# A two-layer graph network kernel: all first-pass dense chunks moved into stage one, layer 0's second half turned into one transposed pass, half of the dst ids looked up

## The reference

```python
h = jnp.maximum(_layernorm(x, axis=-1), 0.0)
x = x + _L0_gnn_ref(h, edge_index, edge_attr_3, edge_weight, ...)   # x + h + out @ w_out
h = jnp.maximum(_layernorm(x, axis=-1), 0.0)
x = x + _L1_gnn_ref(h, ..., src, dst)                               # three layers over (row, col)
...
proj = jnp.einsum('nf,hfg->nhg', x, w_proj)
delta = proj[sender] - proj[receiver]
radial_logits = jnp.einsum('ehf,hf->eh', delta, radial_score) - radial_distance_scale * edge_len[:, None]
tangential_logits = jnp.einsum('ehf,hf->eh', delta, tangential_score)
alpha = e / s[receiver]
return jax.ops.segment_sum(alpha[:, :, None] * delta, receiver, num_segments=num_nodes)
```

## Time and profile before

| | |
|---|---|
| median of 3 runs | 3198.97 us (3197.86 to 3202.41) |
| span of the profiled execution | 3197.3 us (its own time is not listed apart; the median stands 1.7 us above the span) |
| busy: PE, PE weight load | 1780.0 us (56%), 1443.3 us (45%) |
| busy: DVE, ACT, POOL | 2195.2 us (69%), 1068.3 us (33%), 1913.7 us (60%) |
| chain that ended last | POOL 48%, issue 18%, DVE 13%, PE 12% |
| mean granted PE clock | 0.687 of full speed |

### The profile page before, as it was taken

How to read it: one execution, slowest core, us unless ns; L and a number is a source line. 1 busy time by engine, 2 the same in 40 slices (tenths; PEclk the granted TensorE clock), 3 DMA queues, 4 the chain that set the end, 5 groups by cost and what they waited for, 6 DMA issues and landing times.

```text
span 3197.3 us, 34323 instructions
## 1 busy us (share of the span) xinstructions
PE 1780.0 (56%) x8972; PEld 1443.3 (45%) x8972; DVE 2195.2 (69%) x5951; ACT 1068.3 (33%) x2292; POOL 1913.7 (60%) x1844
## 2 busy tenths in 40 slices
PE   1124444441399986653665654665665656655663
PEld 0023333331299975542454433453444544544442
DVE  6748888887877744434555553897866988766775
ACT  0024444442144420001333323553444644443221
POOL 0057777777888017776777775017773017773776
PEclk9975555565555555556777776897888987787555
DMA  0023332231122212214222211233332333333543
GB/s 7 3 54 82 84 88 82 83 86 41 41 86 86 83 60 69 71 50 96 62 63 61 64 40 34 70 85 96 98 104 64 88 88 94 102 98 84 126 119 85
DMA packets 283933, 238.03 MB, mean 74 GB/s; under 512 B 161125, under 2 KB 207611, under 8 KB 283637
## 3 DMA queue, kind: packets, MB, share of 16 engines
q1 hardware_dynamic: 226933, 196.13, 21.4%
q0 software_dynamic: 56832, 40.05, 5.5%
HBM read 163.62 MB, written 84.20 MB: 78 GB/s over the span
## 4 chain that ended last, share of the span: by engine, by line
POOL 48%; issue 18%; DVE 13%; PE 12%; DVEq 4%; DMA 2%; SPq 1%; ACT 1%; POOLq 0%; ACTq 0%
POOL big L1003 13%; POOL G L994 12%; POOL regs L1845 7%; POOL out L1010 6%; POOL regs L1854 5%; PE bank L923 5%; POOL x_after_layer L647 5%; DVE den L1271 3%; PE bank L916 3%; DVE big L1285 2%; DVE big L1591 2%; PE bank L872 1%; DVEq L1590 1%; PE bank L1451 1%; DVEq L1273 1%
## 5 line engine op out<-in xcount | busy, mean ns | idle before, releaser
L1003 POOL DMA_INDIRECT big<-layer_rows,late x392 | 425.9, 1087 | 305.8 <-SPq L1075 186.9
L1845 POOL DMA_INDIRECT regs<-in_x,G x200 | 213.8, 1069 | 234.8 <-DVEq L1711 174.1
L1451 PE MATMUL bank<-regs,SQ 99*128 99x256 bf16 x1764 | 274.8, 319 | 84.2 <-ACT SQ L1357 77.7
L647 POOL DMA_INDIRECT x_after_layer<-G,idx_s x200 | 197.0, 985 | 198.0 <-DVEq L808 135.9
L1870 POOL DMA_INDIRECT farf<-dst_float,VAL x196 | 252.8, 1290 | 59.7 <-issue 59.7
L1451 PEld LDWEIGHTS bank<-regs,SQ 99*128 99x128 bf16 x1764 | 189.3, 112 | 152.8 <-ACT SQ L1357 102.7
L1010 POOL DMA_INDIRECT out<-G,scat_i x196 | 194.7, 993 | 104.4 <-issue 61.4
L1854 POOL DMA_INDIRECT regs<-in_x,G x200 | 211.2, 1056 | 70.2 <-issue 59.7
L1271 DVE SCALAR_TENSOR_TENSOR den<-steps,late,bank 128x256 f32<-128x256 f32 x588 | 245.2, 472 | 9.6 <-PE bank L1451 9.3
L994 POOL DMA_INDIRECT G<-x_after_layer,own_i x196 | 200.6, 1023 | 69.2 <-issue 61.0
L994 POOL DMA_INDIRECT G<-x_after_layer,far_i x196 | 198.5, 1013 | 66.5 <-issue 66.5
(11 more groups left out here) (416 smaller groups left out, 5745.7 us busy)
## 6 DMA issues: line engine op xcount, KB each, us to landing
regs<-x_after_layer SPq DMA_DIRECT2D x96, 256.0 KB, 3.2
out<-regs SPq DMA_DIRECT2D x96, 256.0 KB, 2.1
XC<-row_of_far_degree SPq DMA_DIRECT2D x147, 128.0 KB, 3.4
den<-in_x SPq DMA_DIRECT2D x50, 256.0 KB, 2.7
x_after_layer<-den SPq DMA_DIRECT2D x50, 256.0 KB, 2.0
regs<-tile_nodes SPq DMA_DIRECT2D x50, 256.0 KB, 3.2
layer_rows<-TS SPq DMA_DIRECT2D x98, 128.0 KB, 2.0
regs<-in_x SPq DMA_DIRECT2D x46, 256.0 KB, 2.8
```

The lines of the kernel that those rows point to most:

```text
L647: g.indirect_dma_start(x1_d, bass.IndirectOffsetOnAxis(ap=idx_s[:, b, k:k + 1], axis=0), G[:, b, k, 0, :], None, bounds_check=top, oob_is_ ...
L1003: ahead(g, l, REVERSED, lambda u, l=l: g.indirect_dma_start(far[:, tile_of(u // C, u % C), :], None, xt_d[l - 1], bass.IndirectOffsetOnAxi ...
L1451: ins = pe.matmul(bank[2 + 2 * b + k // 2][:, (k % 2) * 256:(k % 2) * 256 + 256], OH[b][0:RB1 + 1, k * P:(k + 1) * P], TAB[0:RB1 + 1, part ...
L1845: g.indirect_dma_start(GR[:, c % DEEP, k, 0, :], None, a["x"], bass.IndirectOffsetOnAxis(ap=own0[:, c * C + k:c * C + k + 1], axis=0), bou ...
```

## The change

Line numbers of the changed program are its own. The parts:

1. **Dense chunks.** RUN_W is gone and RUN_A has all 98 chunks. Step c of stage one takes `d0` = chunk 2c - 1 and begins `d1` = chunk 2c, which it finishes in step c + 1. Chunks whose number is a multiple of 4 (24 of them, `by_row`) are handled row by row on ACT: eight Square activations of 64 columns with an accumulated sum, one Sqrt, and eight Relu activations with a scale and a bias of their own. DVE then only sums, makes a small reciprocal and product, and adds.
2. **One turned pass.** The weigh pass and the scatter pass become one of 50 steps. The projection is done with `wm` as the stationary side: two matmuls of 512 moving columns, giving 64 features x 512 edge slots. On that turned layout one `tensor_tensor_scan` with a 0/1 mask, in place in PSUM, forms the running sum of each node with the carry of the chunk before; limiting, the projection with w_out (four small matmuls), and the sum with the own rows follow, and POOL scatters from `big2` with the ids in `scat_i`. Same-node matrix, tile ends, carry step and second turn are gone, and so are their DMAs.
3. **dst ids.** POOL fetches 24 of 49 chunks (96 indirect DMAs). The other 25 are looked up inside the pass: every second step ACT makes four one-hot tiles, PE does 16 matmuls of 98 columns, DVE four picks.

```diff
-RUN_IDS = [[*range(NCH)], [*range(NCH, DCH + 2)], [*range(49)], [*range(49, DCH + 2)]]
+RUN_IDS = [[*range(DCH + 2)], [*range(49)], [*range(49, DCH + 2)]]
+FETCHED = 24
+
+
+def dense_of_step(c):
+
+    return (2 * c - 1 if c else 0, 2 * c if 0 < c < NCH - 1 else None)
...
+        def by_row(tag, c):
+            return tag is RUN_A and c > 0 and c % 4 == 0
...
+        def run_second(v, tag, c):
+            n, (_, _, Q_, st), (name, i) = run_parts(tag, c), run_buf(tag, c), lane(tag, c)
+            v.wait_ge(signal(f"{name}_sq"), i + 1)
+            if by_row(tag, c):
+                v.reciprocal(st[0:n, 2], st[0:n, 2])
+                v.drain()
+                ins = v.scalar_tensor_tensor(st[0:n, 1], st[0:n, 0], -1.0 / F, st[0:n, 2], ALU.mult, ALU.mult)
...
+        def run_square(s_, tag, c):
+            n, (X_, C_, Q_, st), (name, i) = run_parts(tag, c), run_buf(tag, c), lane(tag, c)
+            s_.wait_ge(signal(f"{name}_cen"), i + 1)
+            if by_row(tag, c):
+                for r in range(RW):
+                    s_.activation(Q_[0:n, r], X_[0:n, r], ACT.Square, bias=st[0:n, 0, r:r + 1], scale=-float(F), accum_out=st[0:n, 1, r:r + 1])
+                s_.drain()
+                ins = s_.activation(st[0:n, 2], st[0:n, 1], ACT.Sqrt, bias=eps_c[0:n, :], scale=1.0 / F ** 3)
...
+            if by_row(tag, c):
+                for r in range(RW):
+                    ins = s_.activation(C_[0:n, r], X_[0:n, r], ACT.Relu, bias=st[0:n, 1, r:r + 1], scale=st[0:n, 2, r:r + 1])
...
+                norm_first(v, "g", b, rows.rearrange("p c d f -> p (c d) f"))
+                if before:
+                    run_second(v, RUN_A, before)
+                run_first(v, RUN_A, d0)
+                norm_second(v, "g", c, b)
+                run_second(v, RUN_A, d0)
+                norm_third(v, "g", c, b)
...
+                run_third(v, RUN_A, d0)
                 look_dve(v, c + AHEAD)
-                dense_second(v, RUN_A, c, b, P, run_buf(RUN_A, c))
                 if c:
                     scored(c - 1)
-            dense_third(v, RUN_A, NCH - 1, 1, P, run_buf(RUN_A, NCH - 1))
+                if before:
+                    run_third(v, RUN_A, before)
+                if d1:
+                    run_first(v, RUN_A, d1)
...
+            def scan(c):
+                b = c % 2
+                v.wait_ge(signal(f"n_mask{c % 4}"), 16 * (c // 4 + 1))
+                v.wait_ge(signal("m_mm"), c + 1)
+                v.tensor_tensor_scan(bank[4 + b][0:F, :], MB[c % 4], bank[4 + b][0:F, :], CARRY[1 - b] if c else 0.0, ALU.mult, ALU.add).then_inc(signal("n_scan"), 1)
+                v.drain()
+
+            def guard(c):
+                b = c % 2
+                if c >= 2:
+                    v.wait_ge(signal("n_proj"), c - 1)
+                RS = bank[4 + b][0:F, :]
+                v.tensor_copy(CARRY[b], RS[:, 511:512])
+                v.tensor_scalar(GH[b], RS, 0.0, HUGE, ALU.max, ALU.min)
+                v.drain()
+                v.tensor_scalar(RS, RS, 0.0, -HUGE, ALU.min, ALU.max)
+                v.drain()
+                v.tensor_tensor(GH[b], GH[b], RS, ALU.add).then_inc(signal("n_safe"), 1)
...
+            for i in range(NCH + 4):
+                if i + 1 < NCH:
+                    weigh(i + 1, (i + 1) % 2, (i + 1) // 2)
+                if 0 <= i - 2 < NCH:
+                    scan(i - 2)
+                    guard(i - 2)
+                if 0 <= i - 4 < NCH:
+                    renew(i - 4)
+                if i >= 2 and i % 2 == 0 and i // 2 - 1 < len(LOOKED):
+                    seek_dst_dve(v, i // 2 - 1)
...
+                for q in range(2):
+                    ins = pe.matmul(bank[4 + b][0:F, :], wm[:, q, :], ZTs[b][:, q * 512:(q + 1) * 512], start=(q == 0), stop=(q == 1))
+                ins.then_inc(signal("m_mm"), 1)
...
+            staged(NCH, [(0, turn_weighed), (1, project), (3, out_proj), (0, seek)])
```

More of the change, by code:

```diff
@@ L376, in run_need @@
             k = c % DEPTH
-            before = sum(len(range(k, len(ids), DEPTH)) for ids in RUN_IDS[:RUN_IDS.index(tag[2])])
+            before = sum(len(range(k, len(ids), DEPTH)) for ids in RUN_IDS[:"abc".index(tag[0])])
             return 16 * (before + c // DEPTH + 1)
[L380 to L386, removed]
@@ new lines, in seek_dst_act @@
+        def seek_dst_act(s_, e):
+            b = e % 2
+            s_.wait_ge(signal(f"q_in{b}"), 16 * (NCH // 2 + e // 2 + 1))
+            if e >= 2:
+                s_.wait_ge(signal("dl_mm"), e - 1)
+            for h in range(2):
+                s_.activation(SQD[h], EIDD[b], ACT.Square, bias=hotb[:, h:h + 1])
+            s_.drain()
+            for h in range(2):
+                ins = s_.activation(GED[b][h], SQD[h], ACT.Relu, bias=hotb[:, 2:3], scale=-1.0)
+            ins.then_inc(signal("dl_hot"), 1)
@@ new lines, in seek_dst_pe @@
+        def seek_dst_pe(pe, e):
+            b = e % 2
+            pe.wait_ge(signal("dl_hot"), e + 1)
+            if e:
+                pe.wait_ge(signal("dl_sel"), e)
+            for k in range(C):
+                for h in range(2):
+                    for part in range(2):
+                        ins = pe.matmul(bank[3][:, k * COLS:(k + 1) * COLS], GED[b][h][:, k * P:(k + 1) * P], LTD[:, h, part, :], start=(h + part == 0), stop=(h + part == 2))
+            ins.then_inc(signal("dl_mm"), 1)
@@ L641, in L0_pool, with seek_dst_dve @@
+        def seek_dst_dve(v, e):
+            v.wait_ge(signal("dl_mm"), e + 1)
+            for k in range(C):
+                u = C * LOOKED[e] + k
+                ins = v.scalar_tensor_tensor(PICKD[k], steps[:, 0:COLS], VAL0[:, u:u + 1], bank[3][:, k * COLS:(k + 1) * COLS], ALU.is_equal, ALU.mult, accum_out=farf[:, u:u + 1])
+            ins.then_inc(signal("dl_sel"), 1)
         def L0_pool(g, top):
-            def step(c, b, j):
+            run_stored(g, RUN_A)
+            for c in range(NCH):
+                landed = signal(f"n_out{c % 4}")
@@ L875, in L0_pe @@
+            for c in range(NCH):
+                out_t(c)
+                if c % 2 == 0 and c // 2 < len(LOOKED):
+                    seek_dst_act(s_, c // 2)
         def L0_pe(pe):
@@ L942, in out_proj @@
-            def out_proj(c, b, j):
-                pe.wait_ge(signal("n_gt"), c + 1)
-                if not early(c):
-                    pe.wait_ge(signal("n_rows"), c - 1)
-                for q in range(C // 2):
-                    ins = pe.matmul(bank[4 + b][:, q * P:(q + 1) * P], pairs(TS[:, b, 2 * q:2 * q + 2, :]), wo[:, :], start=True, stop=True)
+                        ins = pe.transpose(bank[n_ % 3][:, k * P:(k + 1) * P], Zs[b][:, k, 2 * q:2 * q + 2, :].rearrange("p h f -> p (h f)"), ident[:, :])
@@ L1706, in _ @@
             v.wait_ge(signal("tiles_turned"), 1)
-            v.tensor_copy(node[0][:, :], bank[0][:, 0:T])
             v.tensor_copy(scat_i[0][:, 0:T], bank[1][:, 0:T])
```

476 lines of the change are left out of this document (208 added, 268 removed).

## The result

| | before | after |
|---|---|---|
| median of the runs shown (4 each) | 3198.41 us (3196.19 to 3202.41) | 3073.34 us (3070.59 to 3076.18) |
| span of the profiled execution | 3197.3 us | 3074.3 us (its own time 3076.18) |
| mean granted PE clock | 0.687 | 0.726 |

What follows compares the result with a forecast made beforehand. No engine bounds the whole: POOL sets stage one, PE the weigh pass, POOL the scatter pass. 3197.3 + 128 - 292.5 + 1.3 = 3034.1, and 1.7 to the median: 3036 us, range 3000 to 3140.

Steps and rivals of the forecast that it cites:

- Stage one, +128 us: Stage one grows from 530.4 to 658 us, as DVE takes over more dense chunks; between +94 and +190.
- the wait: Odd steps of stage one: DVE waits 2.0 us for ACT's eight squares and root; bounds 0.6 and 4.6.
- Softmax, 0: The 90.2 us between stage one and the first weigh stay unchanged.
- SP's second load and store per step have a whole step of 13 us to land, so they cost nothing: Stage one: SP's added transfers per step add 0 us.
- The pass, -292.5 us: First weigh to last scatter falls from 590.5 to 298 us, at DVE's 5.6 us per step.
- the PE rival: Joined pass: PE stays at 1.2 GHz, 7.7 us per step, 3139 us in all; chance 0.13.
- the in-place rival: Joined pass: DVE writes in place in PSUM at half rate, 9.4 us per step, 3223 us; chance 0.04.
- I add 0.4, a third of its length: Joined pass: DVE's weigh delays POOL by 0.4 us per step, from 5.14 to 5.54, just under DVE.
- upper bound of 6.4: Joined pass: POOL's four issues take at most 4 x 1.59 = 6.4 us per step.
- 20 us to the first finished rows: Start of the joined pass: 20 us from the first weigh to the first finished rows.
- dst ids: POOL's 96 fetches instead of 196 alone gain nothing, but keep POOL from being 160 us late.
- Layer 1, +1.3: Layer 1 keeps its order; its first root on ACT needs a table load, +1.3 us, or 0 if hidden.

Runs made afterwards that it cites:

- the run with the tails early: Changed kernel with the two tail chunks (106 partitions) at places 1 and 3, not 96 and 97: ratio 0.947 to the kernel before, on a disturbed chip.
- the lookups later: Changed kernel with the pass's dst lookups starting two to four steps later on ACT, PE and DVE: ratio 0.944 to the kernel before, on a disturbed chip.

## Why the prediction was right and where it was short

**Stage one, +128 us: right, +124.** Even steps 12.62 for 12.55, odd steps 14.01 for 14.0, the wait 1.83 for 2.0, a square 0.333 for 0.34. The order of the two engines gave the structure, and the row with 0.292 us for 8 columns gave the size. The estimate of 0.24 us per square that the prediction drew from the Trainium skill, page ScalarE: Activation LUTs (section What ACT_TABLE_LOAD costs), has no reading of the sum in it and would have made the wait 1.2. By the rule of the Trainium skill on the same page (section Rules for kernel authors), to run relu and multiplications on VectorE because it is faster per element, ACT's part should lose. Here DVE is the bound and ACT is not: ACT's part won about 4 us as written, 35 us once DVE asked late (3042.5 against 3077.6 us), and a further 0.70 us a step with all even chunks.

**Softmax, 0: wrong by 8 us.** The step that failed is "SP's second load and store per step have a whole step of 13 us to land, so they cost nothing". The last stores have no step behind them: SP waits for them before the ids, and they were now the two tail chunks, 10.75 us to land where the wait before the change was 2.1 (the run with the tails early shows that it is these). Before, the tail's stores lay at the end of the weigh pass. The Trainium skill, page DMA: Bandwidth & Descriptors (section Why a DMA increments its semaphore by 16 and not by 1), says that a DMA uses the largest number of engines up to 16 that divides the slowest dimension of both its sides, which is two for 106; the DMA share of 0.14 and 44 GB/s, against 0.73 and 271 for 128 partitions, agree.

**The pass, -292.5 us: short by 30.** PE's clock rose as forecast (0.90; eight turns took 1.97 us at 985.5 and 1.10 at 996.8), the scan took 1.27 us and DVE's step 5.50 for 5.6, so neither the PE rival nor the in-place rival came. Two terms were mis-sized.
- "I add 0.4, a third of its length": the stretch is 4 x (1.203 - 0.985) = 0.87 us a step, so POOL, at 6.0 us and not 5.54, set the end. From the first scatter to the last it took 300 us instead of 274 + 4 = 278: 22 us. The row for it was there: fetches of 1.290 us, some 3.9 of them in a 6.15 us step, are 1.2 us of stretch a step; the prediction spread it over all of DVE's work instead of asking what a single weigh does. Its own upper bound of 6.4 held it.
- "20 us to the first finished rows": 27.9 to the first scatter, since PE's first lookups wait for ACT's one-hot tiles, and the second turn and the first projection stand behind them (DVE's fourth weigh waits 5.3 us): 8 us. With the lookups later it is 20.8 us.

**dst ids: right.** The 96 fetches ended at 997.4, 13 us after the first weigh and 15 before the first scatter, and with all 196 the pass is 106 to 124 us longer. That their removal alone is worth nothing was argued and not run.

**Layer 1, +1.3: 7.5.** The table load costs 0.6 us (DVE's first root wait is 0.93 us instead of 0.37). The rest is spread over 1750 us with no place of its own, and the same stretch took 1756.9 to 1761.8 in the four runs on the steady chip; its cause stays open.

## What to carry to other kernels

Before a DVE operation is put beside a queue of indirect DMAs, look at where its operands lie: price each operation with two operands in SBUF at some 0.7 of its length on POOL, once per operation (0.87 us per step for a weigh of 1.21 here), and try to give it one operand from PSUM. That pays until DVE is the next limit: 27 us here. When work goes to an idle engine, count when the busy engine asks for the result: here the same move to ACT was worth 4 us in one order and 35 in another. When work is added to a stage, look at what waits for its last piece, and put the odd-shaped pieces first.

## What the runs showed of the hardware that was not expected

- A weigh of 1.21 us with both operands in SBUF lengthens the issue it meets by 0.82 to 1.18 us; with its weights in PSUM, by nothing (0.982 us on average, 1.03 at most). A 128x256 product with both in SBUF (0.41 us) left 1.018.
- A product that reads its second operand broadcast from PSUM is as long as from SBUF: 1.21 us for 1,024 columns. A scan and a limit of 512 columns in place in a bank took 1.27 and 0.69 us: the time forecast from the rows of before, and that of 512 columns in SBUF.
- Reading out a sum on ACT is an instruction of 0.19 us, and the next square starts 0.09 us behind its start.
- Two stores of 106 partitions (212 KB each), issued together, took 10.75 us to land; the two of 128 partitions (256 KB) issued together 11 us earlier took 2.5.
